# Rows of stationary operands spaced by 2112 bytes, and a reordered start of a one-core transformer layer

## The chip, the core and the metric

One NeuronCore of a Trainium2 chip (trn2) runs the whole program. The metric is the device time of one execution in microseconds, as a median over repeated runs. The kernel is written by hand, engine by engine, with explicit semaphores. In the profile PE is TensorE's matmul stream, PEld its stream of weight loads (the stationary operand), DVE is VectorE, ACT is ScalarE, POOL is GpSimd, SP is SyncE, whose queue here only issues DMAs.

## What is computed

For 16 blocks of 512 tokens with 256 features (8192 rows in all):

- `xn` = layer norm of `x` without scale and bias.
- Linear attention, 16 heads of 16: `q, k, v = xn @ W + b`; `q` and `k` go through `elu + 1`; `kv = k^T v` for each head; `out = q kv / max(q . sum(k), 1e-6)`; then `@ Wo + bo`.
- A mixture of experts: a shared SwiGLU branch `silu(a) * b` of `xn @ w_in.T` (1024 wide), then `@ w_out.T`; a routed branch with one hidden layer for all experts (`w1`, 1024 wide, SwiGLU) and an output matrix for each of 8 experts; a router picks one of two groups and in it the two best experts of four, so a row belongs to one of 12 pairs.
- `x + attention + shared + routed`.

Products are taken in three matmuls of a split operand each: a value is cut into a high part (rounded to the 32-bit format `f32r`) and a low part (the rest), and `hi*hi + hi*lo + lo*hi` is summed in PSUM. `mm3` issues these three.

## The kernel before, in words

**Two phases.** Phase one runs 16 rounds, one for each block of 512 tokens (four tiles `t` of 128 rows, two chunks `c` of 128 features). Phase two runs the routed experts over 75 tiles of 128 rows that have the same expert pair; their hidden rows were scattered to DRAM (`h_d`) in phase one, come back by DMA, are transposed by DVE, split by ACT and DVE, multiplied by the two experts' matrices, weighted by DVE and added to `out` by an indirect DMA of POOL.

**A round on TensorE** (`batch` in the tensor block). In this order: keys and router logits (266 columns) and values (256 columns), tile by tile, with `xnT` stationary and `wk` or `wv` moving; queries (`wq` stationary, `xnT` moving, 512 columns); `hidden(0)` (`win` stationary, `xnT` moving, 512 columns); the small matmuls of `kv`; `hidden(1)`; four times `routed(t)` (`xnT` stationary, `w1` moving, 512 columns) with ranks and normalizer between them; `kvT @ wo` in plain float32; `hidden(2)`, `hidden(3)`; at last the output of the block, `y`, with `h` and `qn` stationary and `wout` and `m` moving (256 columns). Phase two has the transposed hidden rows `rh` stationary (they lie in the rows of `xnT` and of `h`) and `wexp` moving (256 columns, at an address that a register gives). Each engine has its own order, written by hand; semaphores link them.

**Where the buffers lie.** `sb` allocates in the order of the program. `margin` fills up to a multiple of `LINE = 512` bytes, and then the buffers follow one after another. All have a size of a multiple of 512 bytes a partition, with `wk` as the one exception among the matmul operands: its rows are 288 elements, 1152 bytes. So every stationary and every moving operand of TensorE starts at a multiple of 512 bytes, but for `wk`: the two rows of `wk_hi` start at 0 and 128 bytes after such a multiple, those of `wk_lo` at 256 and 384. `pair(name, shape)` allocates a high and a low part.

**The start, before round 0.** SP issues, with nothing between them: two tiles of `x`, `w_k`, all constants that stay (`stay`, whose first 128 columns are the identity for the transposes), `w_q`, the biases, `w_in`, and `c_round` (a triangle and the `spread` matrix); ACT's queue issues the other two tiles of `x`, the router's weights and `w_v`. ACT waits for all three of the key and value loads (`kv_w_ld`), rounds `wk`, the router's and `wv` to their high parts, makes the high parts of the transposed rows (`first_high`), then rounds `wq` and `win`. DVE normalises block 0, makes the low parts of `wk`, of the transposed rows (`first_low`), of `wv` and of `wq` (`low_parts`), and then five small constants behind a wait for `c_ld`, with `const_set` as their signal. POOL computes the reciprocal root, then waits for the high parts of `win` and makes the low parts of `win`, `w1` and `wout`. PE warms up with 64 small matmuls, waits for `stay`, transposes block 0, waits for the low part of `wk` (`w_split` 1), for that of `wv` before the values (`w_split` 2), for that of `wq` before the queries (`w_split` 3). SP, behind its first loads, waits for `xn_rdy` (block 0 is normalised) and issues block 1 and the parts of `w1`. In round 0 the values of tile 2 wait for the first key tile's eviction (`kb_rdy`), which is DVE's `k_in(0)`; PE's `hidden(0)` waits for `ffn_split` 1 and `const_set`, and DVE's `phiq` waits for `ffn_split` 4 (all four parts of `win`'s low half).

Of the kernel before, what the change touches and what calls it, by code (L numbers as in the profile page):

```python
# [6 lines left out]
def layer_program(nc, x, w_k, w_v, w_q, w_o, w_in, w_out, w_exp, w_rt, b_q, b_kl, b_o,  # L7
                  c_stay, c_round, out):

    f32, f32r, bf16, i32 = mybir.dt.float32, mybir.dt.float32r, mybir.dt.bfloat16, mybir.dt.int32  # L10
    ALU = mybir.AluOpType
# [3 lines left out]
    P = 128  # L15
    HP = 32
    QG = P // HP
    B, S, D = 16, 512, 256
    N = B * S
    TB = S // P  # L20
    DC = D // P
    HC = 4
# [13 lines left out]
    H1 = 512  # L36
    HR = H1 + 4
# [11 lines left out]
    with ctx:  # L49
        def sb(name, shape, dt):  # L50
            return ctx.enter_context(nc.sbuf_tensor(name, shape, dt))

        def sem(name):
            return ctx.enter_context(nc.semaphore(name))

        def pair(name, shape):

            return sb(name + "_hi", shape, f32r), sb(name + "_lo", shape, f32r)

        KL = D + 10  # L60
        LINE = 512
        CONSTS = 128
        sb("margin", [P, (LINE - CONSTS) // 4], f32)
        wv_hi, wv_lo = pair("wv", [P, DC, D])
        wq_hi, wq_lo = pair("wq", [P, DC, D])
        win_hi, win_lo = pair("win", [P, DC, 1024])
        wout_hi, wout_lo = pair("wout", [P, HC, D])
        wexp_hi, wexp_lo = pair("wexp", [P, W1 + B * UNIT])
        wo = sb("wo", [P, DC, D], f32)
        wstage = sb("wstage", [P, 1024], f32)  # L70

        xt = sb("xt", [P, TB, D], f32)
        res = sb("res", [P, TB, D], f32)
        xn = xt
        xnT_hi, xnT_lo = pair("xnT", [P, DC, S])
        kb = sb("kb", [P, TB, D], f32)
        relut = sb("relut", [P, 2, 512], f32)
        qn = kb[:, :, :].rearrange("p t n -> p (t n)").rearrange("p (c s) -> p c s", c=DC)
        phiq = sb("phiq", [P, DC, S], f32)
        qn_hi, qn_lo = pair("qn", [P, DC, S])  # L80
        gated = sb("gated", [P, 2, S], f32)
        h_hi, h_lo = pair("h", [P, HC, S])
        m_hi, m_lo = pair("m", [P, DC, D])

        spread = sb("spread", [P, DC, P], f32r)
        kvT = sb("kvT", [P, DC, P], f32)
        wk_hi, wk_lo = pair("wk", [P, DC, D + 32])
        hrow = sb("hrow", [P, TB, H1 + 32], f32)
        expt = hrow[:, 2:4, 0:H1]
        v = sb("v", [P, TB, DC, QG, HP + 1], f32)  # L90

# [1 line left out]
        stay = sb("stay", [P, P + 3 * HP + DC * 32 + NROW + 11], f32)  # L93
# [101 lines left out]
        x_ld = sem("x_ld")  # L195
        x0_ld = [sem(f"x0_ld{t}") for t in range(TB)]
        stay_ld = sem("stay_ld")
        c_ld = sem("c_ld")
        warm_set = sem("warm_set")
        r_ld = sem("r_ld")  # L200
        w_ld = sem("w_ld")

        w_round = sem("w_round")
        w_split = sem("w_split")
        ffn_split = sem("ffn_split")
        w1_split = sem("w1_split")
        const_set = sem("const_set")
# [153 lines left out]
        def _(sp):  # L361
# [3 lines left out]
            def loads(done, pairs, stage):  # L365
                for to, of in [(buf, of) for buf, of, _, _ in stage] + pairs:
                    sp.dma_start(to, of).then_inc(done, 16)
            loads(kv_w_ld, [], stage_kv[0:1])
            sp.dma_start(stay[:, :], c_stay).then_inc(stay_ld, 16)
            loads(q_w_ld, [], stage_q)  # L370
            loads(c_ld, [(bkl[:, :], b_kl), (bq[:, :], b_q)], [])
            loads(in_w_ld, [], stage_in)
            loads(c_ld, [(round_f, c_round)], [])
# [80 lines left out]
        def _(pe):  # L454
            def first_transposes():

                pe.wait_ge(stay_ld, 16)
                for t in range(TB):
                    pe.wait_ge(xn_rdy, t + 1)
                    for c in range(DC):  # L460
                        mm = pe.transpose(bank[2 + 2 * c][:, t * P:(t + 1) * P], phik(t)[:, c * P:(c + 1) * P], ident)
                        if t == TB - 1:
                            mm.then_inc(t_done, 1)
# [27 lines left out]
            def batch(b, last):  # L491

                for t in range(TB):
                    if t == 0:
                        wait(pe, rg_rdy, TB * b)
                    x_hi, x_lo = xnT_hi[:, :, t * P:(t + 1) * P], xnT_lo[:, :, t * P:(t + 1) * P]
                    for c in range(DC):
                        if t == 0:
                            pe.wait_ge(tlo, DC * b + c + 1)
                        mm = mm3(pe, bank[t][:, 0:KL], x_hi[:, c, :], x_lo[:, c, :],  # L500
                                 wk_hi[:, c, 0:KL], wk_lo[:, c, 0:KL], c == 0, c == DC - 1)
                    mm.then_inc(k_done, 1)
                    if first_row(b) and t == 0:
                        pe.wait_ge(w_split, 2)
                    if t == 2:
                        pe.wait_ge(kb_rdy, TB * b + 1)
                    for c in range(DC):
                        mm = mm3(pe, bank[7 if t < 2 else 0][:, (t % 2) * D:(t % 2 + 1) * D], x_hi[:, c, :], x_lo[:, c, :],
                                 wv_hi[:, c, :], wv_lo[:, c, :], t % 2 == 0 and c == 0, c == DC - 1, True)
                    if t % 2 == 1:  # L510
                        mm.then_inc(v_done, 1)

                if first_row(b):
                    pe.wait_ge(w_split, 3)
                for o in range(DC):
                    if o == 1:
                        wait(pe, base_rdy, DC * b - 1)
# [111 lines left out]

            warm_up(WARM)  # L630
            first_transposes()
            pe.wait_ge(w_split, 1)
            rounds(pe, batch, B)

# [39 lines left out]
        def _(act):  # L675
# [38 lines left out]

            def batch(b, last):
                if first_row(b):
                    act.wait_ge(w_split, 3)
                    act.wait_ge(const_set, 1)
                for i in range(2):
                    act.wait_ge(v_done, 2 * b + i + 1)  # L720
# [101 lines left out]
        def _(dve):  # L822
# [309 lines left out]
            def low_parts(stage, n):  # L1132
                for buf, _, hi, lo in stage:
                    n += 1
                    dve.wait_ge(w_round, n)
                    ins = dve.tensor_tensor(lo, buf, hi.bitcast(f32), ALU.subtract)
                ins.then_inc(w_split, 1)

            def transposed(t, g):

# [15 lines left out]
            first_normalise()  # L1156
            low_parts(stage_kv[0:2], 0)
            first_low()
            low_parts(stage_kv[2:3], 2)
            low_parts(stage_q, len(stage_kv))  # L1160
            dve.wait_ge(c_ld, 16 * 3)
            dve.wait_ge(kv_w_ld, 16 * 3)
            dve.wait_ge(stay_ld, 16)
            dve.tensor_scalar(nbq[:, :], bq[:, :], -1.0, None, ALU.mult)
            dve.tensor_copy(triones[:, 0, :], tri_f)
            dve.tensor_copy(spread[:, :, :], spread_f)
            dve.tensor_copy(run[:, :], slot_row)
            dve.tensor_copy(tok[:, :], tok0).then_inc(const_set, 1)
            dve.wait_ge(const_set, 1)
            dve.wait_ge(w_split, 3)  # L1170
            rounds(dve, batch, B)

            def add(t, g, n, to):
# [40 lines left out]
        def _(pool):  # L1214
# [4 lines left out]
            def reciprocal_root(b):  # L1219
                pool.wait_ge(var_rdy, b + 1)  # L1220
                pool.tensor_tensor(rstd[:, :], var[:, :], mhalf[:, :], ALU.pow).then_inc(rstd_rdy, 1)
# [56 lines left out]
                    split(0, W1, UNIT)  # L1278

            reciprocal_root(0)  # L1280
            def cut_in(of, n):
                return [of[:, k * 256:(k + 1) * 256] for k in range(n)]

# [128 lines left out]
```

## Time and profile before

| | us |
|---|---|
| median of 3 runs | 921.02 |
| lowest and highest of them | 920.88, 921.07 |
| the profiled execution, its own time | 922.05 |
| the profiled execution, span of the trace | 920.2 |
| mean granted TensorE clock | 0.996 |

The span runs from the first to the last instruction; the 1.85 us between it and the profiled execution's time lie around it. A row of a group is: line, engine, operation, output and inputs by the program's names (moving operand first, then stationary), shapes, count, and behind the bar the busy time in us, the mean duration of one in ns and the idle time before them. A row of the timeline is: start in us, length in us, engine, line, operation, names, shape, count, and in brackets the idle time before it with what ended it. Matmuls are pipelined: a record of 0.28 us overlaps the next, and what a matmul costs is the distance from its start to the next start.

### The profile page before, as it was taken

The numbers are of one execution on the slowest core, as the hardware profiler recorded it, in microseconds if no ns is written. First come the engines' busy times: TensorE is split into PE (matmuls) and PEld (weight loads), VectorE is DVE, ScalarE is ACT, GpSimd is POOL, SyncE is SP. The second block draws the span as 40 slices with busy tenths as digits, with TensorE's granted clock in tenths as the row PEclk, the third lists the DMA queues.
The fourth block names the chain that finished last, engine by engine and source line by source line (L and its number), as shares of the span: only waits on it lengthen the run. The fifth ranks groups of instructions, "written<-read, shape, count | busy, mean of one in ns | idle before, by whom it ended". The sixth has DMA issues, their size and how long they took to land. (4 is left out here: it accounts for less than half of the span.)

```text
span 920.2 us, 22781 instructions
## 1 busy us (share of the span) xinstructions
PE 903.5 (98%) x6982; PEld 815.6 (89%) x6983; DVE 694.1 (75%) x1816; ACT 367.3 (40%) x605; POOL 403.9 (44%) x486
## 2 busy tenths in 40 slices
PE   8999999999999999999999999999999999999996
PEld 7798988889898989888898989898888999999996
DVE  6878777787868687777878696877676777777773
ACT  5654544353545445443525454453432222222220
POOL 3654342443425243424434243434242666555554
PEclk9999999999999999999999999999999999999999
DMA  6432413132322324141323223241156888888870
GB/s 216 136 116 70 125 51 120 69 103 90 93 100 93 116 69 125 46 125 69 103 80 103 91 92 126 69 125 47 59 204 144 145 143 143 148 137 135 137 128 1
DMA packets 141992, 98.63 MB, mean 107 GB/s; under 512 B 53136, under 2 KB 133008, under 8 KB 141968
## 3 DMA queue, kind: packets, MB, share of 16 engines
q1 hardware_dynamic: 103584, 62.50, 23.7%
q0 software_dynamic: 15920, 25.32, 12.5%
q10 hardware_dynamic: 22464, 10.51, 4.8%
q8 instruction: 13, 0.21, 0.1%
q14 instruction: 11, 0.09, 0.0%
HBM read 53.29 MB, written 46.43 MB: 108 GB/s over the span
## 5 line engine op out<-in xcount | busy, mean ns | idle before, releaser
L350 PE MATMUL bank<-wexp_hi,xnT_hi 128*128 (+1 forms) x560 | 188.1, 336 | 1.5 <-DVE xnT_lo L1149 1.1
L352 PE MATMUL bank<-wexp_hi,xnT_lo 128*128 (+1 forms) x560 | 185.7, 332 | 0.0
L351 PE MATMUL bank<-wexp_lo,xnT_hi 128*128 (+1 forms) x560 | 185.7, 332 | 0.0
L1227 POOL TENSOR_TENSOR h_lo<-gated,h_hi 128x256 fp32r<-128x256 f32 x128 | 98.7, 792 | 141.2 <-ACT h_hi L709 141.2
L350 PEld LDWEIGHTS bank<-wexp_hi,xnT_hi 128*128 128x128 f32 x560 | 106.3, 190 | 15.1 <-issue 4.6
L352 PEld LDWEIGHTS bank<-wexp_hi,xnT_lo 128*128 128x128 f32 x560 | 106.4, 190 | 10.3
L351 PEld LDWEIGHTS bank<-wexp_lo,xnT_hi 128*128 128x128 f32 x560 | 106.4, 190 | 9.5
L350 PE MATMUL bank<-xnT_hi,win_hi 128*128 128x512 f32 x256 | 102.1, 399 | 0.0
L351 PE MATMUL bank<-xnT_lo,win_hi 128*128 128x512 f32 x256 | 100.4, 392 | 0.0
L352 PE MATMUL bank<-xnT_hi,win_lo 128*128 128x512 f32 x256 | 99.6, 389 | 0.0
L1251 POOL TENSOR_TENSOR res<-res,bo_t 128x256 f32<-128x256 f32 x64 | 49.2, 801 | 112.3 <-DMA res<-x 112.3
L1246 POOL DMA_INDIRECT h_d<-hrow,pos_i x64 | 63.0, 985 | 71.8 <-DVE hrow L976 37.5
L350 PE MATMUL bank<-wexp_hi,h_hi 128*128 x296 | 83.9, 283 | 0.1
L351 PE MATMUL bank<-wexp_lo,h_hi 128*128 x296 | 83.8, 283 | 0.0
L352 PE MATMUL bank<-wexp_hi,h_lo 128*128 x296 | 83.8, 283 | 0.0
L709 ACT CAST h_hi<-gated 128x512 fp32r<-128x512 f32 x64 | 39.7, 621 | 102.6 <-DVE gated L972 102.6
L1324 POOL DMA_INDIRECT out<-res,idx_cur x39 | 61.3, 1571 | 43.6 <-DVE res L1178 33.5
L972 DVE TENSOR_TENSOR gated<-gated,bank 128x512 f32<-128x512 f32 x64 | 43.8, 685 | 47.3 <-ACT gated L705 47.3
L350 PE MATMUL bank<-wout_hi,h_hi 128*128 128x256 f32 x256 | 72.5, 283 | 0.0
L351 PE MATMUL bank<-wout_lo,h_hi 128*128 128x256 f32 x256 | 72.4, 283 | 0.0
L352 PE MATMUL bank<-wout_hi,h_lo 128*128 128x256 f32 x256 | 72.4, 283 | 0.0
L1324 POOL DMA_INDIRECT out<-relut,idx_cur x36 | 56.1, 1559 | 33.3 <-DVE relut L1178 22.6
(198 smaller groups left out, 2377.4 us busy)
## 6 DMA issues: line engine op xcount, KB each, us to landing
res<-x SPq DMA_DIRECT2D x16, 512.0 KB, 3.6
out<-res SPq DMA_DIRECT2D x16, 512.0 KB, 2.8
xt<-x SPq DMA_DIRECT2D x15, 512.0 KB, 3.4
xn_d<-xt SPq DMA_DIRECT2D x15, 512.0 KB, 4.9
xt<-xn_d SPq DMA_DIRECT2D x60, 128.0 KB, 2.7
xt<-h_d SPq DMA_DIRECT2D x76, 64.0 KB
xt<-h_d ACTq DMA_DIRECT2D x76, 64.0 KB
kb<-h_d SPq DMA_DIRECT2D x76, 64.0 KB
```

Of the source, the lines that this page charges most:

```text
L350: e.matmul(to, w_hi, m_hi_, start=first_, stop=False, skip_group_check=free)
L351: e.matmul(to, w_hi, m_lo_, start=False, stop=False, skip_group_check=free)
L352: return e.matmul(to, w_lo, m_hi_, start=False, stop=last_, skip_group_check=free)
L709: act.copy(h_hi[:, j, :], gated[:, j % 2, :]).then_inc(hhi_rdy, 1)
L972: dve.tensor_tensor(gated[:, j % 2, :], gated[:, j % 2, :], bank[up_bank][:, :], ALU.mult).then_inc(gate_rdy, 1)
L1227: ins = pool.tensor_tensor(h_lo[:, j, cols], gated[:, j % 2, cols], h_hi[:, j, cols].bitcast(f32), ALU.subtract)
L1246: pool.indirect_dma_start(d, bass.IndirectOffsetOnAxis(ap=pos_i[:, t:t + 1], axis=0), src, None).then_inc(done, 16)
L1251: ins = pool.tensor_tensor(res[:, t, :], res[:, t, :], bo, ALU.add)
L1324: pool.indirect_dma_start(out, bass.IndirectOffsetOnAxis(ap=idx_cur[:, t // TB, t % TB:t % TB + 1], axis=0), ring[t], None, bounds_check=N ...
```

## The change

Three things change. The buffers are allocated in another order, and `xnT` and `h` come from `apart`, which gives each row 528 elements (2112 bytes) for 512 used ones; a filler `aside` of 192 bytes stands before them. The first loads of SP are reordered: the identity is a load of its own with its own semaphore, the query weights and all later loads wait until the three key and value loads have landed. And the low parts of `wv` and `wq` and the five small constants move from DVE to POOL, ahead of POOL's other splits, with semaphores of their own; DVE waits for the value split and for the constants before its first round.

The addresses that follow, each as bytes past a multiple of 512: all of `wv`, `wout`, `wexp`, `wo`, `m`, `wq`, `win` at 0; `wk` as before (0 and 128, 256 and 384); the two rows of `xnT_hi` and of `xnT_lo` at 192 and 256; `qn` at 320; the four rows of `h_hi` and of `h_lo` at 320, 384, 448 and 0. The rows of `hrow` shrink from 544 to 516 elements.

```diff
+        ROW = S + 16
+        def apart(name, n):
+            hi = sb(name + "_hi", [P, n, ROW], f32r)
+            sb(name + "_hi_end", [P, (-n * ROW) % (LINE // 4)], f32)
+            lo = sb(name + "_lo", [P, n, ROW], f32r)
+            return hi[:, :, 0:S], lo[:, :, 0:S]
         sb("margin", [P, (LINE - CONSTS) // 4], f32)
         wv_hi, wv_lo = pair("wv", [P, DC, D])
-        wq_hi, wq_lo = pair("wq", [P, DC, D])
-        win_hi, win_lo = pair("win", [P, DC, 1024])
         wout_hi, wout_lo = pair("wout", [P, HC, D])
         wexp_hi, wexp_lo = pair("wexp", [P, W1 + B * UNIT])
         wo = sb("wo", [P, DC, D], f32)
+        m_hi, m_lo = pair("m", [P, DC, D])
+        wk_hi, wk_lo = pair("wk", [P, DC, D + 32])
+        wq_hi, wq_lo = pair("wq", [P, DC, D])
+        win_hi, win_lo = pair("win", [P, DC, 1024])
...
-        xnT_hi, xnT_lo = pair("xnT", [P, DC, S])
-        qn_hi, qn_lo = pair("qn", [P, DC, S])
-        h_hi, h_lo = pair("h", [P, HC, S])
-        m_hi, m_lo = pair("m", [P, DC, D])
-        wk_hi, wk_lo = pair("wk", [P, DC, D + 32])
-        hrow = sb("hrow", [P, TB, H1 + 32], f32)
+        sb("aside", [P, 192 // 4], f32)
+        xnT_hi, xnT_lo = apart("xnT", DC)
+        qn_hi, qn_lo = pair("qn", [P, DC, S])
+        h_hi, h_lo = apart("h", HC)
+        hrow = sb("hrow", [P, TB, HR], f32)
...
             loads(kv_w_ld, [], stage_kv[0:1])
-            sp.dma_start(stay[:, :], c_stay).then_inc(stay_ld, 16)
+            sp.dma_start(ident, c_stay[:, 0:P]).then_inc(ident_ld, 16)
+            sp.wait_ge(kv_w_ld, 16 * 3)
             loads(q_w_ld, [], stage_q)
+            sp.dma_start(stay[:, P:], c_stay[:, P:]).then_inc(stay_ld, 16)
             loads(c_ld, [(bkl[:, :], b_kl), (bq[:, :], b_q)], [])
...
-                pe.wait_ge(stay_ld, 16)
+                pe.wait_ge(ident_ld, 16)
...
-                        pe.wait_ge(w_split, 2)
+                        pe.wait_ge(v_split, 1)
...
-                    pe.wait_ge(w_split, 3)
+                    pe.wait_ge(q_split, 1)
...
-                    act.wait_ge(w_split, 3)
+                    act.wait_ge(q_split, 1)
                     act.wait_ge(const_set, 1)
...
             first_low()
-            low_parts(stage_kv[2:3], 2)
-            low_parts(stage_q, len(stage_kv))
-            dve.wait_ge(c_ld, 16 * 3)
-            dve.wait_ge(kv_w_ld, 16 * 3)
-            dve.wait_ge(stay_ld, 16)
-            dve.tensor_scalar(nbq[:, :], bq[:, :], -1.0, None, ALU.mult)
-            dve.tensor_copy(triones[:, 0, :], tri_f)
-            dve.tensor_copy(spread[:, :, :], spread_f)
-            dve.tensor_copy(run[:, :], slot_row)
-            dve.tensor_copy(tok[:, :], tok0).then_inc(const_set, 1)
+            dve.wait_ge(v_split, 1)
             dve.wait_ge(const_set, 1)
-            dve.wait_ge(w_split, 3)
             rounds(dve, batch, B)
...
             reciprocal_root(0)
+            pool.wait_ge(xn_rdy, TB)
+            for buf, _, hi, lo, n, done in ((*stage_kv[2], 3, v_split), (*stage_q[0], 4, q_split)):
+                pool.wait_ge(w_round, n)
+                for c in range(DC):
+                    ins = pool.tensor_tensor(lo[:, c, :], buf[:, c, :], hi[:, c, :].bitcast(f32), ALU.subtract)
+                ins.then_inc(done, 1)
+            pool.wait_ge(c_ld, 16 * 3)
+            pool.wait_ge(stay_ld, 16)
+            pool.tensor_scalar(nbq[:, :], bq[:, :], -1.0, None, ALU.mult)
+            pool.tensor_copy(triones[:, 0, :], tri_f)
+            pool.tensor_copy(spread[:, :, :], spread_f)
+            pool.tensor_copy(run[:, :], slot_row)
+            pool.tensor_copy(tok[:, :], tok0).then_inc(const_set, 1)
```

## Rows read from the trace of the kernel before

**Rows 1.** The page, part 1: busy time, share of the span and instructions of each engine.

```profile
PE 903.5 (98%) x6982; PEld 815.6 (89%) x6983; DVE 694.1 (75%) x1816; ACT 367.3 (40%) x605; POOL 403.9 (44%) x486
```

**Rows 2.** Groups of instructions by form, PE, whole span.

```profile
L350 PE MATMUL bank<-xnT_hi,win_hi 128*128 128x512 f32 x256 | 102.1, 399 | 0.0
...
L350 PE MATMUL bank<-wout_hi,h_hi 128*128 128x256 f32 x256 | 72.5, 283 | 0.0
...
L583 PE MATMUL bank<-wo,kvT 128*128 128x256 f32 x64 | 16.4, 378 | 0.0
```

**Rows 3.** Timeline of PE in round 6: 512-column matmuls, then the block's output.

```profile
295.57 1.02 PE L583 MATMUL bank<-wo,kvT 128*128 128x256 f32 x4
...
299.42 0.39 PE L352 MATMUL bank<-xnT_hi,win_lo 128*128 128x512 f32 x1
...
302.14 0.39 PE L352 MATMUL bank<-xnT_hi,win_lo 128*128 128x512 f32 x1
...
302.84 0.28 PE L351 MATMUL bank<-wout_lo,h_hi 128*128 128x256 f32 x1
...
310.88 0.28 PE L352 MATMUL bank<-wout_hi,h_lo 128*128 128x256 f32 x1
```

**Rows 4.** Timeline of PE: keys, values and the first queries of round 7.

```profile
311.74 0.28 PE L350 MATMUL bank<-wv_hi,xnT_hi 128*128 128x256 f32 x1
...
312.45 0.29 PE L350 MATMUL bank<-wk_hi,xnT_hi 128*128 128x266 f32 x1
312.57 0.29 PE L351 MATMUL bank<-wk_lo,xnT_hi 128*128 128x266 f32 x1
312.70 0.28 PE L352 MATMUL bank<-wk_hi,xnT_lo 128*128 128x266 f32 x1
...
313.90 0.29 PE L350 MATMUL bank<-wk_hi,xnT_hi 128*128 128x266 f32 x1
...
316.79 0.39 PE L350 MATMUL bank<-xnT_hi,wq_hi 128*128 128x512 f32 x1
...
317.95 0.39 PE L352 MATMUL bank<-xnT_hi,wq_lo 128*128 128x512 f32 x1
```

**Rows 5.** Busy time by stretch: the start of round 0, and phase two.

```profile
11.12:14.40 3.28, 3.28 (x16) 3.28 (x16) 2.30 (x9) 2.00 (x2) 0.00 (x0) 0.51 1.07 410
...
694.00:910.00 216.00, 215.77 (x1789) 214.88 (x1790) 156.68 (x298) 45.88 (x74) 122.73 (x111) 1.00 0.76 131
```

**Rows 6.** Timeline of all engines, the first 17 us.

```profile
7.86 1.09 PE L461 MATMUL bank<-stay,hrow 128*128 128x128 f32 x8 [1.52 <-DMA stay<-c_stay]
8.01 0.62 ACT L678 CAST wk_hi<-kb 128x512 fp32r<-128x512 f32 x1 [4.10 <-DMA kb<-w_v]
...
10.61 0.36 PE L350 MATMUL bank<-wk_hi,xnT_hi 128*128 128x266 f32 x1 [1.66 <-DVE xnT_lo L878]
...
12.85 0.17 DVE L1164 TENSOR_SCALAR nbq<-bq 128x2 f32<-128x2 f32 x1 [0.59 <-DMA relut<-c_round]
...
13.55 0.42 DVE L983 TENSOR_TENSOR kb<-bank,bkl 128x256 f32<-128x256 f32 x1
...
14.45 0.89 POOL L1295 TENSOR_TENSOR win_lo<-res,win_hi 128x128 fp32r<-128x128 f32 x2 [7.85 <-ACT win_hi L678]
```

**Rows 7.** DMA issues, first 30 us: destination, queue, count, KB, us to landing.

```profile
kb<-w_v ACTq DMA_DIRECT2D x1, 256.0 KB, 5.8
...
relut<-c_round SPq DMA_DIRECT2D x1, 192.0 KB, 7.5
```

**Rows 8.** Timelines of POOL and DVE, 28 to 31 us.

```profile
28.35 0.88 POOL L1295 TENSOR_TENSOR win_lo<-phiq,win_hi 128x128 fp32r<-128x128 f32 x2
...
29.27 1.29 DVE L1017 TENSOR_TENSOR phiq<-hrow,relut 128x512 f32<-128x512 f32 x2
```

**Rows 9.** Waits of PE in round 0 (timeline).

```profile
31.15 0.64 PE L564 MATMUL bank<-phiq,khead 128*32 128x128 f32 x16 [0.74 <-DVE phiq L1017]
...
42.57 0.73 PE L588 MATMUL bank<-qn_hi,spread 128*128 128x512 f32 x2 [1.24 <-DVE qn_hi L1060]
```

More of the change, by code:

```diff
@@ L197, in layer_program @@
         stay_ld = sem("stay_ld")
+        ident_ld = sem("ident_ld")
         c_ld = sem("c_ld")
@@ L203, in layer_program @@
         w_round = sem("w_round")
-        w_split = sem("w_split")
+        k_split = sem("k_split")
+        v_split = sem("v_split")
+        q_split = sem("q_split")
         ffn_split = sem("ffn_split")
@@ L631, in _ @@
             first_transposes()
-            pe.wait_ge(w_split, 1)
+            pe.wait_ge(k_split, 1)
             rounds(pe, batch, B)
@@ L1136, in low_parts @@
                     ins = dve.tensor_tensor(lo, buf, hi.bitcast(f32), ALU.subtract)
-                ins.then_inc(w_split, 1)
+                ins.then_inc(k_split, 1)
             def transposed(t, g):
```

## The prediction, made before the changed kernel ran

> **What bounds the kernel now.** I read the busy table first, then the groups of PE by form, then PE's timeline in a steady round and in phase two, then the first 45 us with all engines. PE's records cover 98% of the span [rows 1], and in phase two 215.77 of 216 us [rows 5]: no other engine has to be made faster, only PE's own pace counts, and its waits in round 0. Since records overlap, the pace is the distance between starts. In [rows 3] twelve 512-column matmuls go from 299.42 to 302.14: 2.72 / 12 = 0.2267 us each; 67 matmuls of 256 columns from 302.84 to 310.88: 8.04 / 67 = 0.120 us each. In phase two it is 216 / 1789 = 0.1207 [rows 5]. The difference of 256 columns costs 0.1067 us, which is 2.4 GHz, one column a cycle; so each width carries the same surplus over its columns, 0.2267 - 0.2133 = 0.120 - 0.1067 = 0.0133 us. It is paid once a matmul, thus once a weight load, and not by the column. Is it a fixed cost of a change of weights? The plain float32 product with `wo` speaks against that: four records in 1.02 us, the last of them 0.378 long [rows 2, 3], give (1.02 - 0.378) / 3 = 0.214 a pass, each with its own load of 128 columns beside it, and hardly a surplus (512 cycles are 0.2133). That pass moves its 256 columns half as fast as an `f32r` matmul, so it walks through memory about as fast as the weight load beside it and doesn't overtake it. The `f32r` stream does, once a load. So the surplus looks like two reads of SBUF in each other's way, and that may depend on addresses.
>
> The keys and values are the only place where the operands' distances differ today (`wk` at 0, 128, 256, 384). There the pace is uneven: twelve matmuls from 312.45 to 313.90, 1.45 us, 0.1208 each with half of them 10 columns (0.004) wider, so 0.1188 brought to 256 columns; the six value matmuls from 311.74 to 312.45 take 0.1183 each [rows 4]. A `wk_lo` one (312.57 to 312.70) takes 0.13. And the first 512-column ones behind them take (317.95 - 316.79) / 5 = 0.232, not 0.2267 [rows 4]. Distances do something, of a few ns and of both signs.
>
> **The layout, part by part.**
> - *256 columns outside keys and values*: 75 x 24 = 1800 in phase two, 48 x 16 = 768 with `wout`, 24 x 16 = 384 with `m`: 2952. Now all operands are at distance 0 and locked at 0.120. After: stationary rows at 192, 256, 320, 384 (phase two), 320, 384, 448, 0 (`h`), 320 (`qn`) against 0. The trace shows no such distance. Bounds: without any surplus 0.107, so 13 ns gained each, -38 us; with that of the dearest `wk_lo` matmul, 0.13 - 0.004 = 0.126, 6 ns lost, +18 us. I take the values' 0.1183, the nearest row of a stream that is knocked out of its even pace by other distances: 1.7 ns x 2952 = -5.0 us.
> - *512 columns*: 6 x 16 x 18 = 1728 (`wq`, `win`, `w1`). Bounds: the 0.214 of the `wo` pass, 1728 x 12.7 ns = -22 us; the 0.232 of the first ones behind the values, 1728 x 5.3 ns = +9 us. Here a gain and a loss have one row each; I take nothing, 0.
> - *Keys and values*: 768, uneven before and after. Bounds 0.107 and 0.126 against 0.1188: -9 and +6 us; I take 0.
> - The other order of allocation, the fillers and the narrower `hrow` add no instruction. ACT, DVE and POOL read and write one row of `xnT` or `h` an instruction, as before. Nothing.
>
> The Trainium skill, "TensorE: Matmul & The Clock Gate", Part 2, step 1, says that TensorE has two independent read ports and that loading the next weights takes no bandwidth from the running matmul. By that rule the three terms are zero. The surplus that the `f32r` matmuls have and the `wo` pass hasn't speaks against it, but doesn't refute it: the formats differ. It is rival C.
>
> **The start, part by part.** The three key and value loads land at 8.0 (ACT starts its cast at 8.01 behind `w_v`, which took 5.8 us) [rows 6, 7]. With `w_q`, most of `stay` and the rest held back, about 1.1 MB of the first loads remain in flight where some 1.6 MB were, and they should land at about 6.4. The transposes no longer wait for `stay` (1.52 us of idle before 7.86) but for the normalised tiles, so they end some 0.5 us earlier; ACT's casts of `wk` and `wv` are over at about 7.8, DVE's low part of `wk` starts when DVE is free. Round 0 starts at about 9.9 in place of 10.61: -0.7 us. But:
> - SP now stands in the wait until 6.4, and seven issues behind it (`w_q`, `stay`, two biases, two halves of `w_in`, `c_round`) shift by 3.8 us. DMA was saturated (1.07 of its capacity at 11 to 14 us, 410 GB/s [rows 5]), so most of that comes back; the engines run empty for about 1 us. `c_round` landed at 12.8 (7.5 us after its issue; DVE waited for it till 12.85) [rows 6, 7]; I take 13.6. Block 1 and `w1`, behind it in SP's queue, shift by 1 to 2 us and have that slack.
> - POOL does two splits of 2 x 0.85 us (two pieces of half that size took 0.88 [rows 8]), the one of `wv` at about 8.1 to 9.8 (values need it at 10.6: hidden; 0.7 us late at most if it runs beside DVE's), the one of `wq` over at about 12.1. Then five constants behind `c_round`, about 1.6 us, twice the 0.7 us from 12.85 to 13.55 in which DVE did them [rows 6]: `const_set` at about 15.2. DVE waits for it before `k_in(0)`, which ran at 13.55 [rows 6]. PE has the first two and a half tiles done at about 13.5, and its values of tile 2 wait for `k_in(0)`: a new stall of about 2.3 us, to 15.8.
> - `win`'s splits, first at 14.45 [rows 6], start at about 15.3. POOL is then at most 0.8 us late down to its last one, which ended at 29.23; DVE's `phiq` started at 29.27 and PE waited 0.74 us for it at 31.15 [rows 8, 9]. PE's lead at the start is covered there: it had waited anyway. DVE has lost 1.7 us of its own, of which it gets back what it waited for PE before. The next wait, at 42.57 [rows 9], is behind DVE again.
> So round 0 ends not earlier but 0.5 us later. Bounds: if all goes as planned, -1; if `c_round` lands 2 us later still, `const_set` and all behind it: +2.5. The clock is open too: from 11.12 to 14.40 it was granted at 0.51, the lower level of 1.2 GHz [rows 5], behind a start with idle PE time (1.66 us before 10.61 [rows 6]); there sixteen matmuls cost some 1.7 us more than at 2.4 GHz. A new stall at 13.5 can move or repeat that stretch: -1.7 to +1.7.
>
> The Trainium skill, "SBUF — State Buffer", Who interferes with whom, says that a VectorE instruction with two SBUF inputs and a GpSimd instruction that reads SBUF block each other for a whole instruction. By it POOL's `wv` split and DVE's low part of `wk` would be in line, not side by side: one 0.8 us piece later at round 0's start, most of which the later waits cover.
>
> **The sum.** -5.0 + 0 + 0 + 0.5 = -4.5 us against the profiled execution's own 922.05 (span 920.2 plus 1.85 around it): 917.5. The median of the runs, 921.02, is 1.03 under the profiled one: 916.5.
>
> **Rivals.**
> A. *The forecast*: other distances give the uneven pace of the values. 916.5, own range 911 to 919.
> B. *The distances are well placed* and the overtaking no longer meets a shared piece of memory. For: the `wo` pass at 0.214. Against: no `f32r` matmul of the trace but single ones goes near it. Half of the two surpluses gone, (38 + 22) / 2 = 30: 921 - 30 + 0.5 = 891; a third gone: 901.
> C. *The layout does nothing* (two ports, a fixed surplus of 13.3 ns): 921.0 + 0.5 = 921.5. For: 0.120 and 0.2267 in all stretches, whatever the multiple of 512. Against: the uneven key stretch.
> D. *The even pace was the good one.* All at distance 0 locks at 0.2267, while 512-column matmuls that come out of a disturbed stretch take 0.232, and `wk_lo` is the dearest at its distance of 256. If the new distances keep the stream out of step, 1728 x 5.3 ns = +9 us, and the 256-column ones give back nothing: 921 + 9 + 0.5 = 930.5; with half of it on 512 and -1.7 ns on half of the others, 923.5. It decides from 1728 x 2.9 ns = 5 us on, a mean pace of 0.2296.
> E. *The change of the start doesn't do what it says*: covered, since its gain is no more than 0.7 us and PE waits at 31.15 and 42.57 anyway. It shifts all the others by -1 to +2.5.
>
> **How the numbers follow.** A 0.38, B 0.17, C 0.17, D 0.28. Two runs of this kernel are told apart from about 0.2%, 1.8 us. A and B are faster by more, but a tenth of A is lost to a worse start; C is mostly the same, D slower but for a tenth: faster 0.53, same 0.17, slower 0.30. The range reaches into B (its third) and to D's full price: 897 to 930.
>
> **What will show it.** The distance between starts of 256-column matmuls in phase two, by tile (`xnT` or `h` stationary): 0.118 for A, 0.120 for C, below 0.115 for B, above 0.120 for D; of `win` and `w1` matmuls 0.2267, under 0.222 for B, 0.23 and up for D. For the start: round 0's first matmul at 9.9; an idle PE before the values of tile 2 that ends with DVE's `kb`; POOL's first constant behind `c_round` at 13.6; PE's wait on `phiq` at 31.15 longer and at the same place or 0.5 us later. The prediction is wrong if the pace is the same for all distances, or moves by more than 3 ns at 256 columns, or if the start moves the second round by more than 2.5 us.

## The result, and the profile after

| | before | after |
|---|---|---|
| median of 4 runs each, on one chip | 921.05 (920.88 to 921.32) | 927.93 (927.59 to 928.48) |
| ratio after / before, 95% interval | | 1.0075 [1.0058, 1.0093] |
| the profiled execution, its own time | 922.05 | 927.59 |
| its span | 920.2 | 925.8 |
| mean granted TensorE clock | 0.996 | 0.994 |

Slower by 0.75%, 6.9 us, where 4.5 us faster was forecast. The two profiled executions differ by 5.5 us. Part 1 of the page after, which answers to [rows 1], says little: nine more instructions on POOL and seven fewer on DVE, and PE still covers 98%.

```profile
PE 906.2 (98%) x6982; PEld 811.9 (88%) x6983; DVE 690.9 (75%) x1809; ACT 367.4 (40%) x605; POOL 408.8 (44%) x495
```

The span has to be cut at fixed instructions: the first key matmul, the first key matmul of each round, the first one of phase two. From PE's records:

| stretch, us | before | after | difference |
|---|---|---|---|
| start to the first key matmul | 10.61 | 9.76 | -0.85 |
| round 0 | 46.75 | 52.02 | +5.27 |
| rounds 1 to 14, each | 42.273 | 42.560 | +0.287, in all +4.0 |
| last round and the gap behind it | 44.75 | 45.35 | +0.60 |
| phase two | 217.34 | 213.85 | -3.49 |
| tail | 8.94 | 8.93 | 0 |

Three terms make it up. A steady round has 108 matmuls of 512 columns; from each one's start to the next start they took 0.401 us longer together (3.7 ns each), 6.4 us in 16 rounds. Its 72 with `wout` and `m` took 0.121 us less, 1.9 us in all; with phase two that is -5.4 us for the 256-column ones. And the start costs 5.27 - 0.85 - 0.29 = +4.1 us. The rest of the rounds gives 0.1 us, the gap ahead of phase two 0.3.

PE's timeline in round 7 of the kernel after, start in us first; it answers to [rows 3]. From the first to the second row are 24 `routed` matmuls, from the third to the fourth 65 of the output.

```profile
338.50 0.39 PE L366 MATMUL bank<-wexp_hi,xnT_lo 128*128 128x512 f32 x1
...
344.07 0.39 PE L366 MATMUL bank<-wexp_hi,xnT_lo 128*128 128x512 f32 x1
...
351.89 0.28 PE L364 MATMUL bank<-wout_hi,h_hi 128*128 128x256 f32 x1
...
359.58 0.28 PE L366 MATMUL bank<-wout_hi,h_lo 128*128 128x256 f32 x1
```

5.57 / 24 = 0.2321 us against 0.2267 before; 7.69 / 65 = 0.1183 against 0.120. The durations are the same as before, 0.39 and 0.28: only distances between starts tell the pace.

Busy time by stretch, after, against [rows 5]: us, then for PE, PEld, DVE, ACT and POOL the busy time and (count), the granted clock, the share of the DMA engines, GB/s.

```profile
5.00:7.50 2.50, 2.50 (x33) 2.33 (x31) 1.22 (x6) 0.47 (x1) 1.05 (x1) 1.00 0.23 81
...
10.00:12.50 2.50, 2.50 (x21) 2.39 (x21) 0.21 (x1) 0.27 (x1) 1.43 (x2) 1.00 0.71 144
...
15.00:17.50 2.50, 0.00 (x0) 0.00 (x0) 0.00 (x0) 1.01 (x2) 0.46 (x3) 0.73 1.04 365
17.50:20.00 2.50, 1.20 (x5) 1.20 (x6) 1.75 (x8) 2.25 (x5) 2.09 (x8) 0.50 1.01 397
20.00:22.50 2.50, 2.50 (x14) 2.50 (x13) 1.48 (x8) 1.41 (x2) 2.50 (x6) 0.50 0.25 93
...
705.00:915.00 210.00, 209.88 (x1772) 209.68 (x1771) 156.78 (x298) 45.46 (x74) 124.23 (x110) 1.00 0.77 133
```

In phase two 210 / 1772 = 0.1185 a matmul, where [rows 5] have 0.1207. At the start the DMA engines run nearly dry at 5 to 7.5 us, then everything comes at once, PE stands still from 15 to 17.5, and behind that its clock is at 0.50, the lower level of 1.2 GHz. Timeline of all engines, after (in brackets the idle time before and what ended it), against [rows 6]:

```profile
7.02 0.33 SPq L381 DMA_DIRECT2D hrow<-w_q  x1
...
9.76 0.36 PE L364 MATMUL bank<-wk_hi,xnT_hi 128*128 128x266 f32 x1 [1.38 <-DVE xnT_lo L894]
...
9.78 0.43 SPq L381 DMA_DIRECT2D relut<-c_round  x1
...
16.49 1.04 ACT L694 CAST win_hi<-res 128x1024 fp32r<-128x1024 f32 x1 [6.22 <-DMA phiq<-w_in]
...
17.04 0.24 POOL L1295 TENSOR_SCALAR nbq<-bq 128x2 f32<-128x2 f32 x1 [5.27 <-DMA relut<-c_round]
...
18.25 0.42 DVE L999 TENSOR_TENSOR kb<-bank,bkl 128x256 f32<-128x256 f32 x1 [8.04 <-POOL tok L1299]
...
18.80 0.58 PE L364 MATMUL bank<-wv_hi,xnT_hi 128*128 128x256 f32 x1 [5.01 <-DVE lg L1000]
```

It reads as one chain: SP is free at 7.02, issues `c_round` at 9.78, and that lands 7.2 us later (against 7.5 in [rows 7]); POOL's constants follow, then DVE's `k_in(0)`, then PE's values of tile 2. Before, the same eviction ran at 13.55, and SP had issued `c_round` at 5.31 (timeline of the kernel before):

```profile
5.31 0.60 SPq L367 DMA_DIRECT2D relut<-c_round  x1
```

Its landing after, from the DMA issues:

```profile
relut<-c_round SPq DMA_DIRECT2D x1, 192.0 KB, 7.2
```

### The profile page after: what moved, and what is told of

It reads as the page before. It is cut to its first block and busy times, and to the rows that moved or that the text cites. A ratio compares the mean times of both kernels' runs of the same rounds, so it can differ in the third digit from the quotient of the medians.

```text
span 925.8 us, 22785 instructions
## 1 busy us (share of the span) xinstructions
PE 906.2 (98%) x6982; PEld 811.9 (88%) x6983; DVE 690.9 (75%) x1809; ACT 367.4 (40%) x605; POOL 408.8 (44%) x495
## 5 line engine op out<-in xcount | busy, mean ns | idle before, releaser
L729 ACT ACTIVATE hrow<-bank 128x512 f32<-128x512 f32 x64 | 38.1, 596 | 85.4 <-PE bank L366 85.4
```

Of the source, the lines that this page charges most:

```text
L729: act.activation(hs[t], bank[gate_bank][:, :], ACT.Silu).then_inc(rsil_rdy, 1)
```

## Experiments

### Which half costs what: `e1_layout_only`, `e2_start_only`

The first has the new buffers with the start of before, the second the buffers of before with the new start (all lines of the diff that touch semaphores, SP and POOL).

> The new layout with the old start. Theory L+S (two additive parts: the layout speeds 256-column matmuls from 0.120 to about 0.118 us and slows 512-column ones from 0.227 to about 0.232, and the start costs by its late constants): phase two 3.5 us shorter, each round 0.29 us longer, round 0 as before; about +1 us against the kernel before, 922. Rival (the start is not the culprit, the layout also slows round 0 or shifts the clock): +4 us or more.

> The old layout with the new start. Theory L+S: steady rounds 42.27 us and phase two as before, round 0 about 5 us longer with PE idle before the values of tile 2, first matmul about 0.9 us earlier: +4.5 us, 925.5. Rival: under +3 us, the rest comes from the layout.

Measured: layout alone 923.62 against 922.35, ratio 1.0007 [0.9992, 1.0022]; its ten runs spread from 920.6 to 926.4. Rounds 1 to 14 take 42.560, as after, phase two 212.76. So the layout gives 4.6 us in phase two and takes 4.6 in 16 rounds. This trace is of the fastest of the ten runs (920.60), and its granted clock was 1.00 all through round 0, where the kernel before had 0.51 from 11.12 to 14.40 us.

Start alone 925.03, ratio 1.0029 [1.0019, 1.0038]: first key matmul at 9.98, round 0 51.23. The timeline of the kernel with the new start alone repeats the chain of after:

```profile
17.95 0.42 DVE L988 TENSOR_TENSOR kb<-bank,bkl 128x256 f32<-128x256 f32 x1 [7.53 <-POOL tok L1288]
...
18.51 0.52 PE L353 MATMUL bank<-wv_hi,xnT_hi 128*128 128x256 f32 x1 [4.49 <-DVE lg L989]
```

The two differences, +1.3 and +2.7 us, sum to 4.0 where after has 6.9; their intervals reach 5.5 together, its own begins at 5.3. The layout's is the less certain. Within the traces the start agrees, +3.9 (9.98 + 51.23 against 10.61 + 46.75) in one kernel and +4.1 in the other, and so do rounds 1 to 14. The whole spans do not add up: 918.8 and 923.0 are -1.4 and +2.8 against 920.2, together 1.4, where after has 5.6. Of the missing 4.2 us 1.5 lie ahead of the second round and 1.5 in phase two. There the tiles in the first row of `h` took 136 cycles a matmul in the trace of the layout alone and 141 in that of after, at the same addresses. So the sizes of the halves are known to one or two us, and that the two parts simply add up is not shown.

### What in the start costs it: `e12_start_round_first`, `e14_start_no_wait`

Both have the layout of before and the new start. In the first `c_round` is issued behind `w_q`; in the second SP doesn't wait.

```diff
             loads(q_w_ld, [], stage_q)
+            loads(c_ld, [(round_f, c_round)], [])
...
             loads(in_w_ld, [], stage_in)
-            loads(c_ld, [(round_f, c_round)], [])
```

```diff
-            sp.wait_ge(kv_w_ld, 16 * 3)
```

> The old layout and the new start, but with the load of c_round right behind the query weights instead of behind w_in. Theory K (the whole loss of the new start is the late const_set, which stands behind c_round): c_round lands at about 11 instead of 17, PE's stall before the values of tile 2 falls from 5 us to under 1, TensorE's clock may stay up, round 0 ends near 57 as before or 0.5 to 1 us earlier: 920 to 921.5. Rival (w_in is late as well, by the wait before the query weights, and takes the place of the constants): PE waits later, before hidden(0), and the time is 923 or more.

> The old layout and the new start without SP's wait for the key and value loads; all else of the new start kept. Theory W (the wait is what costs; POOL's splits and constants are about neutral): c_round lands at about 13 again, const_set at about 14.3, PE waits under 1 us before the values of tile 2, 920.5 to 922. Rival (POOL's work in front of its splits of win costs by itself): round 0 over 1 us longer than before, 922.5 or more.

Earlier `c_round`: 923.95, ratio 1.0037 [1.0022, 1.0051], nothing won; the rival of the expectation was right. The constants come at 11.76 and PE no longer stops at the values of tile 2, but now `w_in` is late, and with it POOL's splits (timeline of that kernel):

```profile
11.76 0.24 POOL L1284 TENSOR_SCALAR nbq<-bq 128x2 f32<-128x2 f32 x1
...
18.06 0.88 POOL L1304 TENSOR_TENSOR win_lo<-res,win_hi 128x128 fp32r<-128x128 f32 x2 [5.19 <-ACT win_hi L683]
```

PE waits 2.0 us for `wexp_lo` and 2.0 for `phiq` later in round 0, and the clock is at 0.72 over 34 to 40 us. Without SP's wait: 921.72, ratio 0.9996 [0.9986, 1.0005], round 0 47.02. The constants on POOL run 4.1 us earlier than in `e2_start_only`, and `k_in(0)` is back at 13.83 (13.55 before):

```profile
12.63 0.24 POOL L1283 TENSOR_SCALAR nbq<-bq 128x2 f32<-128x2 f32 x1 [0.73 <-DMA relut<-c_round]
...
13.83 0.42 DVE L987 TENSOR_TENSOR kb<-bank,bkl 128x256 f32<-128x256 f32 x1 [3.13 <-POOL tok L1287]
```

So the wait in SP's queue is the whole loss, 925.03 - 921.72 = 3.3 us. POOL's new work and the loads' new order cost nothing that can be told from the noise.

### Which rows of the layout: `e3_h_only`, `e4_shift_only`

Both have the start of before; the diffs are against the kernel after. The first keeps `xnT` at 0 with rows of 2048 bytes, and only `h` (320, 384, 448, 0) and `qn` (320) lie aside. The second has rows of 2048 bytes throughout: `xnT` all at 192, `qn` and all of `h` at 320.

```diff
-        sb("aside", [P, 192 // 4], f32)
-        xnT_hi, xnT_lo = apart("xnT", DC)
+        xnT_hi, xnT_lo = pair("xnT", [P, DC, S])
+        sb("aside", [P, 320 // 4], f32)
```

```diff
-        ROW = S + 16
+        ROW = S
...
+        sb("aside2", [P, 128 // 4], f32)
```

> The old start; xnT back on multiples of 512 bytes with rows of 2048, only h and qn at the new distances. Theory L+S, with the two widths wanting different things: 512-column matmuls lock at 0.2267 again, the output of a block keeps 0.118, and in phase two the tiles that lie in h keep 0.118 while those in xnT go back to 0.120: about 2 us from the rounds and 1.5 to 2 us from phase two, 917 to 917.5. Rival (the uneven pace of the 256-column stretch carries over into the 512-column one and costs there what it gave): within 1 us of the kernel before.

> The old start and the new layout, but rows 2048 bytes apart again: xnT as a whole at 192 bytes, qn and h at 320. If the distance alone sets the pace, as with the layout alone (about 922). If it is the 64 bytes between rows that keep the stream out of step, a constant distance locks into an even pace as distance 0 does, 0.120 and 0.2267 or another pair of values: within 1 us of the kernel before, or a clear change with an even pace.

With `h` alone: 918.05, ratio 0.9948 [0.9931, 0.9964]. The 512-column matmuls are back at 272 cycles and a round takes 42.113. Constant offsets: 910.75, ratio 0.9872 [0.9855, 0.9888]. PE's timeline of that kernel, `hidden(0)` and the output of a round, then its window of phase two:

```profile
319.10 0.39 PE L361 MATMUL bank<-xnT_hi,win_hi 128*128 128x512 f32 x1
...
321.67 0.40 PE L363 MATMUL bank<-xnT_hi,win_lo 128*128 128x512 f32 x1
...
345.22 0.28 PE L361 MATMUL bank<-wout_hi,h_hi 128*128 128x256 f32 x1
...
352.59 0.28 PE L363 MATMUL bank<-wout_hi,h_lo 128*128 128x256 f32 x1
```

```profile
695.00:895.00 200.00, 199.48 (x1751) 198.82 (x1750) 156.97 (x296) 45.46 (x74) 121.58 (x109) 1.00 0.80 140
```

2.57 / 11 = 0.2336: `hidden` is dearest at distance 192, 280 cycles. The output takes 7.37 / 65 = 0.1134 (136 cycles), phase two 200 / 1751 = 0.1142. So there is a better pace for 256 columns, 136 cycles, which the mixture of rows in the changed kernel did not reach. For 512 columns the distances of this run are bad, though constant: its queries run evenly at 280. The dearer pace of 512 columns is thus not a matter of being out of step.

### Both good at once, first try: `e6_x0_h320`

`xnT` at 0 for the 512-column matmuls, `qn` and `h` all at 320, rows of 2048 bytes, against the kernel after:

```diff
-        xnT_hi, xnT_lo = apart("xnT", DC)
+        xnT_hi, xnT_lo = pair("xnT", [P, DC, S])
+        sb("fill1", [P, 320 // 4], f32)
...
-        h_hi, h_lo = apart("h", HC)
+        h_hi, h_lo = pair("h", [P, HC, S])
```

> Old start; every row again 2048 bytes after the one before, xnT at 0, qn and h at 320. Theory P (a constant distance locks into an even pace that depends on the distance and the width: 256 columns take 0.1133 us at 320 bytes and 0.120 at 0, 512 columns take 0.2267 at 0): 24 output and 48 hidden-output matmuls a round gain 6.7 ns less (0.48 us a round, 7.6 in all), half of phase two 6 ns each (5.6 us): 908. Rival (the pace of one stretch is set by what runs before it, so the gain of the run with everything shifted is not to be had in parts): 914 or more.

A miss: 917.77, ratio 0.9954 [0.9937, 0.997]. The same distance for the output as in `e4_shift_only`, yet (timeline, then window of phase two)

```profile
343.83 0.28 PE L349 MATMUL bank<-wout_hi,h_hi 128*128 128x256 f32 x1
...
351.49 0.28 PE L351 MATMUL bank<-wout_hi,h_lo 128*128 128x256 f32 x1
```

```profile
695.00:905.00 210.00, 209.52 (x1758) 209.01 (x1759) 156.11 (x296) 45.29 (x73) 123.76 (x109) 1.00 0.78 133
```

7.66 / 65 = 0.1178, 141 cycles and not 136. The distance alone doesn't set the pace: in `e4_shift_only` the output comes behind matmuls at 280, here behind matmuls at 272.

### The map of distances: `e5_x320`, `e7_x128`, `e8_x448`, `e11_sub`

Rows of 2048 bytes, `wq` and the moving weights at 0. Offsets: `e5_x320`: `xnT` 320, `win` 192, `h` 384. `e7_x128`: `xnT` 128, `win` 64, `h` 256. `e8_x448`: `xnT` 448, `win` 192, `h` 64. `e11_sub`: `xnT` 32, `win` 16, `h` 96. In all four `qn` lies at the offset of `h` (384, 256, 64, 96), and not at the 320 that three of the expectations name. Each by fillers like those above; that of `e5_x320`:

```diff
         wq_hi, wq_lo = pair("wq", [P, DC, D])
+        sb("fill1", [P, 192 // 4], f32)
         win_hi, win_lo = pair("win", [P, DC, 1024])
...
+        sb("fill2", [P, 128 // 4], f32)
+        xnT_hi, xnT_lo = pair("xnT", [P, DC, S])
+        sb("fill3", [P, 64 // 4], f32)
```

> Old start; xnT at 320, wq at 0, win at 192, qn at 320, h at 384, rows 2048 apart. A scan of distances (moving less stationary, modulo 512): queries 320, hidden 128, routed 192, phase two 192 (tiles in xnT) and 128 (tiles in h). Theory P says that the distance alone decides, whichever operand is shifted: queries about 0.229 as the routed matmuls had at 320, routed 0.2333 as the queries had at 192, phase two 0.1133 for the tiles in xnT. Rival (the absolute address decides): the queries and routed matmuls keep the paces they had with xnT at 192.

> Old start; xnT at 128, wq at 0, win at 64, qn at 320, h at 256, rows 2048 apart. Distances: queries 128, hidden 64, routed 384, phase two 384 and 256. Theory P: an even pace in each stretch; the queries here equal the hidden matmuls of the run with xnT at 320 (both 128). Rival: they differ.

> Old start; xnT at 448, wq at 0, win at 192, qn at 320, h at 64, rows 2048 apart. Distances: queries 448, hidden 256, routed 64, phase two 64 and 448. Theory P: an even pace in each stretch; the routed matmuls here equal the hidden ones of the run with xnT at 128 (both 64). Rival: they differ, and shifting a moving operand isn't the same as shifting a stationary one.

> Old start; xnT at 32, wq at 0, win at 16, qn and h at 96, rows 2048 apart: distances that are no multiple of 64 (queries 32, hidden 16, routed 480, phase two 480 and 416, output 416). If memory is cut in pieces of 64 bytes the paces lie at or between those of the neighbouring multiples (512 columns 272 to 280 cycles, 256 columns 136 to 144). Rival: operands that don't start on a piece need one more of them, and every matmul here is slower by some cycles than at either neighbour.

These are single runs, one of each: 921.0, 926.04, 916.18, 923.67. They were made for the distances between starts by stretch, in cycles. The table has the pace that a stretch settles into in the steady rounds and in phase two; what comes behind "as" repeats matmul by matmul:

| distance, bytes (modulo 256) | 512 columns | 256 columns |
|---|---|---|
| 0 | 272, even (`e8_x448`, `hidden`: 448 - 192) | 144, even (`e7_x128`, output: 0 - 256) |
| 64 | 275, as 278 271 275 (`e5_x320` queries, `e7_x128` `hidden`, `e4_shift_only` and `e8_x448` `routed`) | 136 or 141 |
| 128 | 278 to 280, uneven (`e5_x320` `hidden`, `e7_x128` queries) | 142.4, as 146 144 143 138 141 (`e5_x320` output) |
| 192 | 280 (`e4_shift_only` and `e8_x448` queries even, `e5_x320` `routed` also as 277 283) | 136 or 141 |
| 16 (`e11_sub`) | 280, uneven (`hidden`) | |
| 32 and 224 (`e11_sub`) | 32: as at 64 (queries); 224: as at 192 (`routed`) | 224: 136 to 137 (phase two) |
| 160 (`e11_sub`) | | 142 (phase two), 144 as 141 144 147 (output) |

It repeats every 256 bytes, and at multiples of 64 it is the distance that counts and not where either row lies: four layouts with different absolute rows give 275 at 64, as theory P of the expectations had it. `e11_sub` bears out neither theory in full: 32 and 224 run as their neighbours 64 and 192, but 16 is dearer than both 0 and 64. Distance 0 is best for 512 columns and, with 160 in one stretch, worst for 256.

### Distance 64 or 192 with 0 kept: `e9_odd64`, `e10_odd192`

`xnT`, `qn`, `h`, `wq`, `win` and the `w1` part of `wexp` at 0; `wout`, `m`, `wv`, `wk` and the experts' part of `wexp` at 64 in the first, 192 in the second. In the second, `SKIP` is 48 and the fillers are larger.

```diff
+        SKIP = 16
+        sb("fill1", [P, 64 // 4], f32)
...
+        wexp_hi = sb("wexp_hi", [P, W1 + SKIP + B * UNIT], f32r)
...
-                            off = at[n] + (W1 + j * D)
+                            off = at[n] + (W1 + SKIP + j * D)
```

> Old start; xnT, wq, win, w1, qn and h at 0; wout, m, wv, wk and the experts' part of wexp at 64, rows 2048 apart. So all 512-column matmuls are at distance 0 and all 256-column ones at 64 (wk at 64, 192, 320, 448). Theory Q (what the scans show: the pace repeats every 256 bytes; 512 columns take 272 cycles of 1.2 GHz at 0 or 256 and 275 to 280 elsewhere; 256 columns take 144 at 0 or 256, 143 at 128, and at 64 and 192 either 136 or 141, by where the stream comes in): phase two at 136 to 137, 12 us less; the output at 136 or 141, 8 or 3 us less; keys and values perhaps 3 us less: 898 to 906. Rival (136 needs 512-column matmuls at the odd distances as well): phase two above 140, 912 or more.

> As the run with 64, but 192 for wout, m, wv, wk and the experts' part. Theory Q gives the same range, 898 to 906; the state in which the output runs, 136 or 141, can differ from the run with 64, since it depends on the entry. Rival: as there.

Both missed the 898 to 906 of their expectation, and the rival was right: 916.05, ratio 0.9946 [0.993, 0.9963], and 912.66, ratio 0.9898 [0.9878, 0.9917]. PE's timeline in the output of a round, and phase two, both of the first:

```profile
343.50 0.28 PE L356 MATMUL bank<-wout_hi,h_hi 128*128 128x256 f32 x1
...
351.16 0.28 PE L358 MATMUL bank<-wout_hi,h_lo 128*128 128x256 f32 x1
```

```profile
695.00:905.00 210.00, 208.90 (x1772) 208.50 (x1770) 157.42 (x298) 45.28 (x73) 124.54 (x110) 1.00 0.77 132
```

Again 141 cycles in the output, 142 in phase two, at either distance; 512 columns at 272. A constant odd multiple of 64 that follows the even pace runs in the dearer state. The distance does not fix the state: in phase two of `e10_odd192` three tiles of 24 matmuls run at 136, then all others at 141, at 192 throughout. What phase two of `e4_shift_only` and of `e8_x448` have, both at 136 to 137, is a step from one odd distance to another (64 to 192). It is not the only way in: in `e5_x320` tiles at 192 run at 136 to 137 between tiles at 128.

### The step between two odd distances: `e13_two_odd`, `e15_both`

512-column operands at distance 0. Output and phase two alternate between 64 and 192: `wout`, `m` and the experts at 64, `qn` at 128, rows of `h` 2176 bytes apart and so in turn at 128 and 0 (modulo 256); phase two uses rows 0 and 2 of `h` beside `xnT`; `wv`, `wk` at 192. The start is that of before. `e15_both` adds the new start without SP's wait.

```diff
+        qn_hi, qn_lo = pair("qn", [P, DC, S])
+        h_hi = sb("h_hi", [P, HC, S + 32], f32r)[:, :, 0:S]
+        h_lo = sb("h_lo", [P, HC, S + 32], f32r)[:, :, 0:S]
```

> Old start. xnT, wq, win, w1 at 0; wout, m and the experts' part at 64; qn at 128; the rows of h 2176 bytes apart at 128, 256, 384, 0; phase two uses xnT's rows and rows 0 and 2 of h. So 512 columns run at distance 0, and 256 columns always at 64 or 192 modulo 256, with steps between the two inside each stretch. Theory R (a step between two odd distances brings the stream into the 136-cycle pace): output 136 to 137 and phase two 137: 5 us and 8 us less than with 192 alone, 898 to 900. Rival (the pace is inherited from the 512-column stretch): both stay at 141, 911 to 912.

> The layout of the run with two odd distances and the new start without SP's wait. If layout and start add up, its time is that of the layout run plus what the start without the wait differs from the kernel before. Rival: the round's pace after another start settles in another state, and it differs by more than 2 us from that sum.

Measured: 903.65, ratio 0.9797 [0.9777, 0.9816], and 903.07, ratio 0.9793 [0.9776, 0.9811]. That is 18.7 and 19.3 us below the kernel before, the best of all. The first missed the 898 to 900 of its expectation, though both paces came as its theory R had them. The second is the sum of the two parts within 0.1 us; the start adds nothing that can be told. Timeline and phase two of the first:

```profile
329.19 0.39 PE L357 MATMUL bank<-wexp_hi,xnT_lo 128*128 128x512 f32 x1
...
334.63 0.39 PE L357 MATMUL bank<-wexp_hi,xnT_lo 128*128 128x512 f32 x1
...
342.36 0.28 PE L355 MATMUL bank<-wout_hi,h_hi 128*128 128x256 f32 x1
...
349.73 0.28 PE L357 MATMUL bank<-wout_hi,h_lo 128*128 128x256 f32 x1
```

```profile
690.00:890.00 200.00, 200.00 (x1756) 199.85 (x1756) 156.76 (x296) 45.35 (x73) 123.73 (x108) 1.00 0.80 140
```

5.44 / 24 = 0.2267, 7.37 / 65 = 0.1134, 200 / 1756 = 0.1139: the best of each width in one kernel.

## Why the prediction was wrong

- **256 columns outside keys and values: right, in part by luck.** -5.0 us forecast, -5.4 measured. The row chosen, the values' 0.1183, is what `y` shows after, though it was of matmuls at distance 0 and no row at the new distances was there. After, it is the mean of distances between 135 and 147 cycles; other layouts with moved rows gave 0.1134, 0.1178 or 0.1199 in the output. Its lower bound, no surplus at all, was never met: 136 cycles are 0.1133 against 0.107.
- **512 columns, taken as 0: failed, +6.4 us.** "Here a gain and a loss have one row each; I take nothing, 0." The loss had the nearer row: an `f32r` matmul with its 512 columns, knocked out of step, at 0.232 [rows 4]; `routed` shows 0.2321 after. That the two are alike is luck. The 0.232 of before is over after five matmuls, at distance 0, and then 0.2267 returns; after, the pace never returns, and `e4_shift_only` shows it dear (275, 280) at constant distances too. The gain rested on the `wo` pass, another format, and its 0.214 was met by no layout. The two weren't of equal weight. With 6.4 in place of 0 the sum would have been 922.9, just under rival D's lower time of 923.5; the measured 927.9 lies between its 923.5 and its 930.5 only with the loss of the start. D was right for 512 columns in that distance 0 is the good one, not in its reason, the lost step; A was right for 256.
- **Keys and values, taken as 0: right.** They took 6947 cycles a round before and 6952 after.
- **The start, +0.5: failed, +4.1.** Right were the earlier first key matmul (9.9 forecast, 9.76 measured; 10.03 to 11.23 in the twelve traces with the old start), the place of the new stall and its chain. Wrong was the step "so most of that comes back ...; I take 13.6": `c_round` came at 17.0. SP was free at 7.02 and not at 6.4, and issued `c_round` at 9.78, 4.5 us later than before (5.31). I had counted on saturated DMA queues that get back what SP lost. But while SP waited, the engines moved 81 GB/s, and the loads that piled up behind were then served together, 1.00 of capacity from 12.5 us on. The 192 KB issued seventh behind the wait took 7.2 us to land, where they had taken 7.5: of the 4.5 us only 0.3 came back. `const_set` came at 18.15, not 15.2, and PE stood for 5.0 us and not for 2.3. The bound of +2.5 was too narrow for the same reason. The clock fell too, within the 5.0 us of idle PE, and was at 0.50 from 17.5 to 22.5 us, where before it was at 0.51 behind 1.66 us. That explains little of the 4.1: PE worked only from 18.80 on, some 4 us at the lower level against 3.3 before, and each costs about half its length (an estimate), so under 0.5 us more. Six of the twelve traces with the old start have such a stretch in their first 20 us, six have none; it is a good part of the scatter between traces. `e14_start_no_wait` shows the wait as the cause, and `e12_start_round_first` that one other order behind it does not help.
- **Rival C, a fixed surplus: wrong**, and with it, for this format, the rule of the Trainium skill ("TensorE: Matmul & The Clock Gate", Part 2, step 1) that loading the next weights takes no bandwidth from the running matmul, so far as the runs can tell: with the same instructions, addresses alone move a 256-column matmul between 136 and 144 cycles. **Rival B, well placed** was wrong for this layout but right in kind: `e13_two_odd` reaches 903.65. It has what the changed layout has not, distance 0 for 512 columns and an alternation of two odd distances for 256.
- **Rival E** was too mild: not a gain that is covered, but a loss.
- **POOL beside DVE: seen, and small.** In `e12_start_round_first` POOL's split of `wv` took 1.82 us where it takes 1.43 after, and DVE's short low part of `wk` beside it 0.73 us where it takes 0.17 after; the first key matmul came at 10.14 and not at 9.76. In `e14_start_no_wait` that low part is over as POOL's split starts, and both take their usual time. DVE's timeline in the first of the two:

```profile
8.66 0.73 DVE L1141 TENSOR_TENSOR wk_lo<-relut,wk_hi 128x20 fp32r<-128x20 f32 x1
```

The sum by measured terms: -5.4 + 6.4 + 0.1 (the rest of the rounds) + 0.3 (the gap ahead of phase two) + 4.1 = +5.5, against 5.6 of the spans. The medians differ by 6.9; the other 1.3 us are not in these two traces.

What stays open: whether the two reads share a piece of the memory, and which; why the 136 state is entered in some places and left in others, and why two traces with the same addresses differ in it; why a steady round of `e2_start_only`, `e12_start_round_first` and `e14_start_no_wait` takes 42.233, 0.04 us less than before, with the same layout.

## What to carry to other kernels

When PE is busy all the time, measure the distance between matmul starts by operand pair, and treat the address distance between moving and stationary rows, modulo 256 bytes, as a parameter for each width by itself; a mixture of rows at several distances gave a pace between the good and the bad. When the trace offers a bound from the same kind of instruction and one from another kind, the term is not zero: take the same kind. Don't hold a queue back to favour one load before asking what lies last behind the wait and who needs it: it pays for the time in which the DMA engines run empty.

## What the runs showed of the hardware that was not expected

- The even paces are multiples of 0.833 ns, and the surplus over the columns depends on operand distance: 8 (136), 13 (141) or 16 (144) cycles at 256 columns, 16 (272), 19 (275) or 24 (280) at 512.
- The pace has memory: at distance 192 the output runs at 136 cycles behind a stretch at 280 (`e4_shift_only`) and at 141 behind one at 272 (`e6_x0_h320`), and keeps it to the end of its 72 matmuls. The state can also change at one distance: phase two of `e10_odd192` begins at 136 and goes on at 141.
- Each change of operand kind costs a few uneven matmuls, as 277 283 274 280 277 before 272 returns (`e13_two_odd`, and the kernel before alike).
